# Householder reduction beside a layer norm: the square root alone on GpSimd, part of the next reflector earlier, the matrix in two copies

## The reference

```
Ln = dinv[:, None] * (diag(degv) - A) * dinv[None, :]
_, U = eigh(Ln)
h0  = relu(layernorm(x))
out = relu(einsum('vn,bvd->bnd', U, h0) @ W1 + b1) @ W2 + b2
z   = nonlocal_attention(out) + out          # theta, phi, g, softmax over 512 keys, batch norm
x + einsum('nv,bvd->bnd', U, z) + z
```

## Time and profile before

| | us |
|---|---|
| median of three runs (lowest to highest) | 3352.58 (3351.86 to 3355.92) |
| the profiled execution | 3354.83 |
| its span in the trace | 3353.1 |
| busy in the span: PE / DVE / ACT / POOL | 3181.8 / 2289.5 / 2413.1 / 1949.6 |

### The profile page before, as it was taken

The page is one execution under the profiler, slowest core; times in us unless marked ns, Lnnn a source line. Parts: engine busy times, 40 slices in busy tenths (PEclk is TensorE's granted clock), DMA queues, the critical chain, the costliest instruction groups (busy, mean ns, idle before and its releaser), DMA issues.

```text
span 3353.1 us, 65817 instructions
## 1 busy us (share of the span) xinstructions
PE 3181.8 (95%) x16040; PEld 2554.4 (76%) x16040; DVE 2289.5 (68%) x6009; ACT 2413.1 (72%) x4380; POOL 1949.6 (58%) x2073
## 2 busy tenths in 40 slices
PE   6888886799999999999999999999999999999997
PEld 5667776677777777777777777778777777777775
DVE  7777778866666666666666666666666666666664
ACT  6888998856666766666666667666666676666665
POOL 4333321146666666666666666666666666666665
PEclk9999999989999999999999999999999999999998
DMA  3333433312222222222222222222222222222222
GB/s 95 93 96 98 105 107 95 95 37 72 74 75 75 73 71 71 71 71 72 73 74 72 71 71 71 71 71 71 73 74 74 75 71 71 71 71 71 73 74 67
DMA packets 111576, 256.22 MB, mean 76 GB/s; under 512 B 47501, under 2 KB 49798, under 8 KB 111494
## 3 DMA queue, kind: packets, MB, share of 16 engines
q1 hardware_dynamic: 111493, 255.25, 27.8%
HBM read 190.69 MB, written 63.44 MB: 76 GB/s over the span
## 4 chain that ended last, share of the span: by engine, by line
PE 80%; DVE 10%; POOL 3%; issue 3%; ACT 3%; DVEq 0%; POOLq 0%; ACTq 0%
PE ps_M L800 8%; PE ps_M L801 8%; PE ps_M L802 8%; PE ps_S L877 7%; PE ps_E L800 7%; PE ps_O L800 7%; PE ps_E L801 7%; PE ps_O L802 7%; PE ps_E L802 7%; PE ps_O L801 7%; PE ps_M L861 3%; POOL sc L450 1%; ACT junkx L537 1%; DVE u L1031 1%; DVE rown L1029 1%
## 5 line engine op out<-in xcount | busy, mean ns | idle before, releaser
L503 POOL TENSOR_TENSOR p_lo<-p,p_hi 128x512 fp32r<-128x512 f32 x1024 | 1380.9, 1349 | 932.1 <-ACT p_hi L654 929.9
L649 ACT ACTIVATE p<-ps_E 128x512 f32<-128x512 f32 x1024 | 613.6, 599 | 332.6 <-PE ps_E L802 307.5
L1394 DVE TENSOR_REDUCE nmx<-ps_S 128x1 f32<-128x512 f32 x1024 | 658.8, 685 | 127.8 <-PE ps_S L877 124.7
L654 ACT ACTIVATE p_hi<-p 128x512 fp32r<-128x512 f32 x1024 | 647.2, 632 | 32.6
L800 PE MATMUL ps_E<-o_hi,Q_hi 123*128 123x512 f32 x1024 | 427.0, 417 | 0.0
L800 PE MATMUL ps_O<-p_hi,v_hi 128*121 128x512 f32 x1024 | 407.2, 398 | 4.2 <-POOL p_lo L503 4.2
L802 PE MATMUL ps_O<-p_lo,v_hi 128*121 128x512 f32 x1024 | 406.7, 397 | 0.0
L801 PE MATMUL ps_E<-o_hi,Q_lo 123*128 123x512 f32 x1024 | 404.4, 395 | 0.0
L801 PE MATMUL ps_O<-p_hi,v_lo 128*121 128x512 f32 x1024 | 404.4, 395 | 0.0
L802 PE MATMUL ps_E<-o_lo,Q_hi 123*128 123x512 f32 x1024 | 404.2, 395 | 0.0
L1374 DVE TENSOR_REDUCE gf<-ps_M 128x256 f32<-128x512 f32 x256 | 177.1, 692 | 261.8 <-PE ps_M L802 261.8
(11 more groups left out here) (363 smaller groups left out, 5947.7 us busy)
## 6 DMA issues: line engine op xcount, KB each, us to landing
rbc<-r_dram SPq DMA_DIRECT2D x128, 484.0 KB
xin<-in_x_dram SPq DMA_DIRECT2D x128, 480.0 KB, 4.2
xt<-in_x_dram SPq DMA_DIRECT2D x128, 480.0 KB, 4.9
out_dram<-y SPq DMA_DIRECT2D x128, 480.0 KB, 3.7
o_hi<-mrow SPq DMA_DIRECT2D x256, 2.0 KB
dcol<-y SPq DMA_DIRECT2D x128, 4.0 KB, 2.0
r_dram<-rcol SPq DMA_DIRECT2D x128, 4.0 KB, 1.4
W1s<-in_L_gnn_W_dram SPq DMA_DIRECT2D x1, 512.0 KB, 4.1
```

Source lines behind the costliest of these rows:

```text
L503: pool.tensor_tensor(p_lo[:, c % 4, :], p[:, c % 4, :], p_hi[:, c % 4, :].bitcast(F32), ALU.subtract).then_inc(plo_sb, 1)
L649: act.activation(p[:, c % 4, :], ps_E[c % 2][:, :], ACT.Exp).then_inc(p_sb, 1)
L654: act.activation(p_hi[:, c % 4, :], p[:, c % 4, :], ACT.Copy).then_inc(phi_sb, 1)
L1394: dve.tensor_reduce(nmx[:, c:c + 1], ps_S[SBANK[c]][:, :], AX.X, ALU.max, negate=True).then_inc(max_sb, 1)
```

## The change

POOL keeps only the root, and gets a new one: `TWICE`, a doubled and gated first element of the factor. DVE makes sign and gates itself, in a group `sign()` of four small instructions behind the `QA` update. The row copy is multiplied by the sign while it is copied, and z uses `ROOT` in place of `DU`. The gate goes into `cu` and the small products L1020 and L1022 are gone. The first part of the next reflector (`i_part`) now reads z before it is finished and the row straight from PSUM; a pair term (`PAIR`) takes what is missing, so `i_part` needs the second factor `zs` no more; it stands behind it in the queue. `QA` is read from one half and written to the other, by turns; at the end the even columns are copied over. Constants of PE's written order change too.

```diff
     row1 = eb("row1", [1, N])
+    zt = eb("zt", [1, N])
     rown = eb("rown", [1, N])
...
 s2_ready = sem("s2_ready")
-du_ready = sem("du_ready")
-gate_ready = sem("gate_ready")
+root_ready = sem("root_ready")
+sign_ready = sem("sign_ready")
+rec_ready = sem("rec_ready")
+twice_ready = sem("twice_ready")
 w_ready = sem("w_ready")
...
-        pool.wait_ge(u_ready, k + 1)
-        chain(pool.tensor_scalar(sc[:, SGN:SGN + 1], u[:, 1:2], 0.0, 2.0, ALU.is_ge, ALU.mult))
-        chain(pool.tensor_scalar(sc[:, SGN:SGN + 1], sc[:, SGN:SGN + 1], -1.0, None, ALU.add))
         pool.wait_ge(s2_ready, k + 1)
-        chain(pool.tensor_tensor(sc[:, ROOT:ROOT + 1], sc[:, S2:S2 + 1], sc[:, 11:12], ALU.pow))
-        pool.tensor_tensor(sc[:, DU:DU + 1], sc[:, SGN:SGN + 1], sc[:, ROOT:ROOT + 1], ALU.mult).then_inc(du_ready, 1)
-        pool.tensor_scalar(sc[:, GATE:GATE + 1], sc[:, XN:XN + 1], TINY, -1.0, ALU.is_gt, ALU.mult).then_inc(gate_ready, 1)
+        pool.tensor_tensor(sc[:, ROOT:ROOT + 1], sc[:, S2:S2 + 1], sc[:, 11:12], ALU.pow).then_inc(root_ready, 1)
+        if k + 1 < STEPS:
+            pool.wait_ge(rec_ready, k + 1)
+            pool.tensor_scalar(sc[:, TWICE:TWICE + 1], u[:, 1:2], sc[:, REC:REC + 1], sc[:, GATE2:GATE2 + 1],
+                               ALU.mult, ALU.mult).then_inc(twice_ready, 1)
...
         pe.wait_ge(xcol_ready, k + 1)
-        mm(ps_V[0:33, 0:L], XI[:, k + 1:k + 34], QA[:, k:N], start=True, stop=True).then_inc(ry_ready, 1)
+        mm(ps_V[0:33, 0:L], XI[:, k + 1:k + 34], QA[:, par * N + k:par * N + N], start=True, stop=True).then_inc(ry_ready, 1)
         behind = max(placed, wanted - LN_BEHIND)
...
+    def sign():
+
+        i_ge = did(TS(s_(SGN), u[:, 1:2], 0.0, 2.0, ALU.is_ge, ALU.mult))
+        did(TS(s_(GATE), s_(XN), TINY, -2.0, ALU.is_gt, ALU.mult))
+        did(TS(s_(GATE2), s_(XN), TINY, -4.0, ALU.is_gt, ALU.mult))
+        need(i_ge)
+        TS(s_(SGN), s_(SGN), -1.0, None, ALU.add).then_inc(sign_ready, 1)
+
     dve.tensor_copy(u[:, 1:N], QA[0:1, 1:N]).then_inc(u_ready, 1)
     dve.wait_ge(u_ready, 1)
     norm(N)
+    sign()
     def reflect(k):
         L = N - k
         par = k % 2
         cu = cs[:, par, N:2 * N]
-        z_ = lambda i: zs[:, N + i:N + L]
+        dve.wait_ge(root_ready, k + 1)
+        dve.wait_ge(sign_ready, k + 1)
+        i_u = did(STT(out=u[:, 1:2], in0=s_(ROOT), scalar=s_(SGN), in1=u[:, 1:2], op0=ALU.mult, op1=ALU.add))
         dve.wait_ge(ry_ready, k + 1)
-        i_row = did(dve.tensor_copy(row1[:, k:N], ps_V[32:33, 0:L]))
-        dve.wait_ge(du_ready, k + 1)
-        i_u = did(T(u[:, 1:2], s_(DU), u[:, 1:2], ALU.add))
-        need(i_row)
-        i_z = did(STT(out=z_(0), in0=row1[:, k:N], scalar=s_(DU), in1=ps_V[0:1, 0:L], op0=ALU.mult, op1=ALU.add))
+        i_row = did(TS(row1[:, k:N], ps_V[32:33, 0:L], s_(SGN), None, ALU.mult))
         need(i_u)
         i_uu = did(STT(out=srow[:, k:k + 1], in0=u[:, 1:2], scalar=u[:, 1:2], in1=s_(XN), op0=ALU.mult, op1=ALU.add))
+        need(i_row)
+        i_z = did(STT(out=zt[:, 0:L], in0=row1[:, k:N], scalar=s_(ROOT), in1=ps_V[0:1, 0:L], op0=ALU.mult, op1=ALU.add))
+        need(i_uu)
+        dve.reciprocal(s_(REC), srow[:, k:k + 1]).then_inc(rec_ready, 1)
         need(i_z)
-        i_dot = did(STT(out=sqj[:, 0:L], in0=u[:, 0:L], scalar=1.0, in1=z_(0), op0=ALU.mult, op1=ALU.mult,
+        i_dot = did(STT(out=sqj[:, 0:L], in0=u[:, 0:L], scalar=0.5, in1=zt[:, 0:L], op0=ALU.mult, op1=ALU.mult,
                         accum_out=s_(AC)))
-        need(i_uu)
-        i_rec = did(dve.reciprocal(s_(REC), srow[:, k:k + 1]))
-        dve.wait_ge(gate_ready, k + 1)
-        need(i_rec)
-        i_rg = did(T(s_(RG), s_(REC), s_(GATE), ALU.mult))
-        need(i_rg)
-        i_ac = did(T(s_(AC), s_(AC), s_(RG), ALU.mult))
-        i_cu = did(TS(cu[:, 0:L], u[:, 0:L], s_(RG), 2.0, ALU.mult, ALU.mult))
-        need(i_ac)
-        STT(out=z_(0), in0=u[:, 0:L], scalar=s_(AC), in1=z_(0), op0=ALU.mult, op1=ALU.add).then_inc(w_ready, 1)
+        dve.wait_ge(rec_ready, k + 1)
+        i_cu = did(TS(cu[:, 0:L], u[:, 0:L], s_(REC), s_(GATE), ALU.mult, ALU.mult))
+        need(i_cu)
+        need(i_dot)
+        STT(out=zs[:, N:N + L], in0=cu[:, 0:L], scalar=s_(AC), in1=zt[:, 0:L], op0=ALU.mult, op1=ALU.add).then_inc(w_ready, 1)
+        now, then = par * N, (1 - par) * N
         if k + 1 < STEPS:
-            need(i_cu)
-            dve.wait_ge(w_ready, k + 1)
-            need(did(STT(out=rown[:, k + 2:N], in0=z_(2), scalar=cu[:, 1:2], in1=row1[:, k + 2:N],
-                         op0=ALU.mult, op1=ALU.add)))
-            STT(out=u[:, 1:L - 1], in0=cu[:, 2:L], scalar=zs[:, N + 1:N + 2], in1=rown[:, k + 2:N],
+            i_part = did(STT(out=rown[:, 0:L - 2], in0=zt[:, 2:L], scalar=cu[:, 1:2], in1=ps_V[32:33, 2:L],
+                             op0=ALU.mult, op1=ALU.add))
+            dve.wait_ge(twice_ready, k + 1)
+            i_pair = did(STT(out=s_(PAIR), in0=s_(TWICE), scalar=s_(AC), in1=zt[:, 1:2], op0=ALU.mult, op1=ALU.add))
+            need(i_part)
+            need(i_pair)
+            STT(out=u[:, 1:L - 1], in0=cu[:, 2:L], scalar=s_(PAIR), in1=rown[:, 0:L - 2],
                 op0=ALU.mult, op1=ALU.add).then_inc(u_ready, 1)
             dve.wait_ge(u_ready, k + 2)
+            dve.wait_ge(w_ready, k + 1)
             norm(L - 1)
             dve.wait_ge(up_ready, k + 1)
-            STT(out=XI[:, k + 2:k + 3], in0=ps_up[0:N, 2:3], scalar=QA[:, k + 1:k + 2],
+            STT(out=XI[:, k + 2:k + 3], in0=ps_up[0:N, 2:3], scalar=QA[:, now + k + 1:now + k + 2],
                 in1=strict[:, k + 1:k + 2], op0=ALU.add, op1=ALU.mult).then_inc(xcol_ready, 1)
-            dve.wait_ge(xcol_ready, k + 2)
         dve.wait_ge(up_ready, k + 1)
-        T(QA[:, k:N], QA[:, k:N], ps_up[0:N, 1:L + 1], ALU.add).then_inc(a_ready, 1)
+        dve.wait_ge(a_ready, k + 1)
+        T(QA[:, then + k:then + N], QA[:, now + k:now + N], ps_up[0:N, 1:L + 1], ALU.add).then_inc(a_ready, 1)
+        if k + 1 < STEPS:
+            sign()
         dve.tensor_copy(wyCT[0:N, k:k + 1], ps_up[0:N, 0:1]).then_inc(c_kept, 1)
     for k in range(STEPS):
         reflect(k)
     dve.wait_ge(a_ready, STEPS + 1)
+    need(did(dve.tensor_copy(QA[:, 0:STEPS:2], QA[:, N:N + STEPS:2])))
     dve.wait_ge(filled, 1)
...
 PARAMS = 15
-XN, S2, ROOT, GATE, SGN, REC, DU, RG, AC = range(9)
+XN, S2, ROOT, GATE, GATE2, SGN, REC, PAIR, AC, TWICE = range(10)
 UNITS = 12
 TAIL_AT = B
-LN_RATE, LN_LEAD, LN_BEHIND = (9, 1), 2, 2
-GRID_AT = 98
-WY_SLOT, WY_STEPS = 96, 19
+LN_RATE, LN_LEAD, LN_BEHIND = (9, 1), 2, 3
+GRID_AT = 99
+WY_SLOT, WY_STEPS = 94, 19
 WY_T, WY_G = 1, 3
...
```

## The result

The changed kernel takes 3341.83 us, the median of seven runs (3340.28 to 3345.68). Seven runs of the kernel before on the same chip give 3353.88 (3351.86 to 3358.72). The ratio is 0.9964, 95% interval 0.9952 to 0.9975: 12.05 us faster. The way was forecast right, and the time lies in the range (3296 to 3350), also in the narrower one of the main case (3316 to 3344). The forecast gain of 23 us was about twice the real one, and the 3341.8 are nearer to the rival with 3350 than to the 3330 of the forecast. The profiled execution took 3345.68 us with a span of 3343.9.

A forecast was written before the change was run, and what follows sets the result against it. It took the steps to be bound by a loop of small dependent instructions. Terms: -20.5 (0.175 us times 117 steps) + 0.3 - 2.9 = -23.1 us, giving 3330 us as median, range 3296 to 3350.

The forecast's parts named there:

- the main case: Whole kernel: the summed terms hold, 3330 us with its own range 3316 to 3344; chance 0.70.
- the rival with 3350: Steps: row copy at its upper bound and sign at the middle pitch cancel the gain; 3350 us, chance 0.09.
- What bounds the kernel: Householder steps: a loop of small dependent instructions sets the pace, 3.72 us a step; no engine is full.
- The change of `u`: In a step, behind root and sign: starts at +1.49 us instead of +1.79, gain 0.30.
- the slower rival: DVE's four sign instructions delay the change of `u`: step 0.12 us longer, 3365 us; decides from pitch 0.13; chance 0.07.
- Row copy and z: After the change of `u`: both held, z ends at +2.37; 0.88 us instead of 0.44, loss 0.44.
- From z's end to the second factor's: Small products and double wait go: 0.70 us instead of 1.09, gain 0.39 a step.
- From there to the next `u`: Second factor's end to the write of `u`, by part and pair term: 0.45 us instead of 0.40, loss 0.05.
- Slope with length: Gain per step near 0.05 us at length 120, 0.20 at 48, 0.29 at the end.
- Holding: DVE: a PSUM read at another partition group waits until DVE is empty, 0.10 us a time, at four places.
- The rival without it (3290 us): The four PSUM reads overlap as others do: step 3.15 us at length 48, 3290 us; chance 0.14.
- The end: Last step to main loop: `GRID_AT` 99 cuts the MJ wait from 11.5 to 7 us; gain 2.9 us.

The follow-up runs named there:

- The experiment with one wait: Changed kernel with the sign's wait before the root's at the change of `u`, and only the pair term's wait at the next `u`: 3334.98 us, ratio 0.9940.
- the kernel that removes the cause: Changed kernel with the matrix row from its own matmul on partition 0, so no PSUM read of the step changes partition group: 3303.84 us, ratio 0.9847.
- Two experiments: `LN_BEHIND`, `GRID_AT` and `WY_SLOT` taken back on the changed kernel, 3343.53 us; their new values put alone on the kernel before, 3352.83 us.

## Why the prediction was right in its way and off in its size

**What bounds the kernel.** Right. The loop of small instructions sets the steps, and what they save arrives at the main loop (11.98 us) and in the time (12.05). That these two agree so closely is partly chance: the first is from one execution, whose own time fell by 9.15. The main loop's start, named as a sign at near 644 us, came at 655.35.

**The change of `u`, forecast 0.30 earlier at +1.49.** Measured +1.45. The root ends at +1.37, and the sign, with its pitch of 0.06 to 0.07, at +1.34 (forecast 1.39). The mechanism was right too: the sign is what releases `u`, 0.11 us behind its end, since its wait is the second one. So what the slower rival named is there, DVE late in front of the root's use, but small: the pitch is far from the 0.13 from which it was to decide.

**Row copy and z, forecast +2.37.** Measured +2.35, a loss of 0.46 against 0.44 forecast. The row copy takes 0.26 us at length 51, inside its bounds (0.20 to 0.31), and not the 0.23 taken.

**From z's end to the second factor's, forecast 0.70.** Measured 0.77. This is the first step that failed in size: `cu` was priced at L1023's 0.23 us of before, with one pointer and one constant. The changed line has two pointers and takes 0.29. The trace of before had no such instruction on DVE, and the bounds named no price for it. The experiment with a constant gives 7.3 us of usual steps for it.

**From there to the next `u`, forecast 0.45.** Measured 0.52. The second step that failed: the two waits in front of L1042 were priced as one, 0.04, though the prediction had read 0.11 for L1017 to L1020 from the same rows and used it at the change of `u`. The experiment with one wait gives 6.0 us. Its other edit takes something back in the late steps, so the single wait by itself may be worth more.

Together -0.04 + 0.02 + 0.07 + 0.07 make the 0.12 between 3.52 and 3.64, so at this length the account closes. Over all 117 steps it closes less well. The forecast gain was 20.5 and the usual steps show 11.1, so 9.4 are missing, 0.08 a step and not 0.12. The two causes are worth 13.3 by experiment. The earlier change of `u` gives back 4.7 at 0.04 a step, and row copy and z take 2.3 at 0.02. That makes 10.9, 1.5 us more than is missing, from sums of single executions and from terms that need not be the same at every length.

**Slope with length.** Right in direction, with a hollow near the start: the gain of the usual step is 0.11 at the 2nd, -0.03 at the 12th, 0.07 at the 50th, 0.13 at the 90th, 0.24 at the 116th. Start and end of the steps, forecast at 4.1 to 4.2 and 3.2, were 4.36 and 3.25.

**Holding.** Right, and it was the disputed reading, from one row. The rival without it (3290 us) is wrong for this kernel. Its size is shown by the kernel that removes the cause: 38 us, where the rival had 40.

**Two copies, `LN_BEHIND`, even columns.** The even columns' copy was priced at 0.3 us with the last step, `LN_BEHIND` at nothing, and the copies by the wait between XI and `QA` that goes. For the copies no gain is shown on the kernel before, and on the changed one it is open. `LN_BEHIND` is right within 2 us. The even columns' copy was not tried alone.

**The end, forecast -2.9, MJ near 7 us.** Measured -3.1 and 6.4 us. Two experiments confirm it in the stretch.

In sum, -11.1 of usual steps, +2.3 of irregular ones and -3.1 at the end make the 11.9 us by which the main loop starts earlier. The forecast had -20.5 + 0.3 - 2.9. The cancelling rival (3350 us) named the row copy and the pitch of the sign; half of a cancelling did happen, but by other terms. The time lies in the range because the range was wide: the mechanism and the way of each part were right, the sizes of two terms were not. The profiled execution gained 9.15 and not 12, since its main loop took 2688.6 us against 2685.8, code that the change doesn't touch.

## What to carry to other kernels

In a chain of small instructions on DVE, look at the partition at which each reads PSUM: a result that lands on the same group as its neighbour's saved 0.10 us a place and 38 us in all, three times what the whole change gained. Price an instruction by a row with the same kinds of operands, and a wait by a row with the same number of waits. Where two waits stand in front of one instruction, write the one that comes true last first, or leave the other out if it is covered.

## What the runs showed of the hardware

- A PSUM read on DVE at another partition group than the last one (32 after 0 or 0 after 32) starts 0.02 to 0.03 us after the instruction in front has ended; at the same group it starts 0.07 to 0.08 before.
- A `TENSOR_SCALAR` on one partition takes 0.273 to 0.352 us with two pointer scalars, 0.213 to 0.274 with one and a constant. POOL's small one (L453) took 0.34 with two pointers and 0.26 with one and a constant, in the kernel with the guard in the square sum.
- A DVE instruction with one semaphore wait, or with two of which the one written first comes true last, starts 0.03 to 0.04 us after the end of what it waits for (the change of `u` with the row on partition 0, 105 of 118 steps). If the one written second comes true last, it starts 0.10 to 0.11 after (116 of 118 steps in the changed kernel, 117 with the waits in the other order).
- The part out of PSUM takes 0.26 us at 49 elements, out of SBUF 0.25 at 50. The 62 cycles more for a PSUM source, which the Trainium skill gives (VectorE: DVE Perf Modes, TRN2 errata), are not there: the trace disagrees.
- Four 1x1 instructions of 0.13 us that wait for nothing follow each other at 0.06 to 0.07 us.
